# Top-32 attention: the mask of every head item from ScalarE's Sign, the flag checked in the next item's last search step

## The chip, the core and the metric

The kernel runs on one core of one Trainium2 chip. The metric is the device time of one launch in microseconds; its median over three runs is 2931.31 us (2930.16 to 2934.05). The core has TensorE (PE, matrix products), VectorE (DVE), ScalarE (ACT), GpSimd (POOL) and SyncE (SP, which starts transfers). Each engine works through its own list of instructions in order; the lists meet only in semaphores.

## The reference, cut to what matters

Four batches of 512 tokens (256 wide) pass four layers: a cross-attention with 16 heads, a mixture of eight experts, a second cross-attention block, and a self-attention with gated values. The change concerns the attention inside the third layer. For each batch and each of four heads, every token scores 1601 context rows and keeps the 32 largest:

```
Q = (x_text @ Wq).reshape(Bb, Tt, H, DH)
K = (x_vision @ Wk).reshape(Bb, Gg, H, DH)
scores = jnp.einsum('bthd,bghd->bhtg', Q, K) / np.sqrt(DH).astype(np.float32)
scores = jnp.where(vision_mask[:, None, None, :], scores, -jnp.inf)
topv, topi = jax.lax.top_k(scores, K_TOP)
probs = jax.nn.softmax(topv, axis=-1)
bi = jnp.arange(Bb)[:, None, None, None]
hi = jnp.arange(H)[None, :, None, None]
ti = jnp.arange(Tt)[None, None, :, None]
attn = jnp.zeros_like(scores).at[bi, hi, ti, topi].set(probs)
attn_mean = attn.mean(axis=1)
V = x_vision @ Wv
c_t = jnp.einsum('btg,bgd->btd', attn_mean, V)
c_t = c_t * text_mask[..., None]
```

The rest of the layer (a film modulation, a long convolution by a discrete Fourier transform, a feed-forward net, layer norms) follows it and is not touched.

## The kernel before

The attention is worked in **items**. A batch has four tiles of 128 tokens, and with four heads 16 items, n = 0 to 15, tile n // 4 and head n % 4. A token is a partition, the 1601 scores of a head lie along the free axis. The order on each engine is written out by hand; per batch a semaphore gets a fixed number of increments, and `nth(b, sem, k)` is its value at the k-th of batch b.

An item passes the engines like this.

- **TensorE** computes scores in steps of half a pair of heads (`scores`, lines 1549 and 1552), four steps ahead of the item. ScalarE copies them to `s_sb` (`score_out`, line 1053).
- **VectorE** searches the scores for the 32 largest in two stages. `search(n, k)`, line 2331, takes the eight largest of 27 parts of 60 scores, in seven portions k = 0 to 6; these 216 candidates are those of the *next* item. Between the portions, the loop over k takes the eight largest of the candidates of the *present* item (line 2346) and strikes them out (line 2348), alternately: four times the one, three times the other. After k = 6 the last of the 32 is the threshold `least`.
- For an **even** item, VectorE works out a bias from the threshold (lines 2361 to 2364: `NEG`, minus the row's maximum, and `under`, minus the number just below the threshold). ScalarE makes the mask with the function Sign (line 1095): +1 where a score reaches the threshold, -1 elsewhere, and the row sum with it. For an **odd** item VectorE makes the mask itself (line 2370), 1 or 0, with the row sum; of the threshold only `NEG` is computed (line 2366).
- **ScalarE** also computes the exponentials of all 1601 scores (line 1090), those of the 32 largest with their sum (line 1096), and, in `scale_head` (line 1073), Relu of the masked exponentials times the weight.
- **TensorE** adds the row sums over the partitions (`count`, line 1563). ScalarE copies the number to `kept` (line 1101): it is the **flag**. If all rows kept exactly 32, the mask is good.
- **VectorE** reads the flag into a register (`settle`) and branches; a slow repair stands in the branch. Then `weight` (lines 2317 and 2319) computes the weight from the sum.
- **GpSimd** multiplies the exponentials by the mask (line 847) as soon as the weight is there, and adds scaled heads to the mean over the heads (line 839). For items 14 and 15 VectorE does this work itself (lines 2381 and 2383).
- When a tile's four heads are added up, TensorE turns the mean (line 1573), ScalarE copies it (lines 874 and 870, in items 7, 11 and 15 and once behind the loop), and TensorE multiplies it with v (line 1581) in two parts; ScalarE copies the result (line 1057).

Where the flag is checked differs. The flag of an even item n is checked at the end of item n+1, behind VectorE's mask. The flag of an odd item n is checked in item n+1 at k = 4. ScalarE writes the flag before `scale_head` in odd items and behind it in even items. Buffers: `s_sb` has six slots, `probs1` three, `kept01` (the mask) and `kept_by_row` two, `under` one.

## Time and profile before

| | |
|---|---|
| Median of three runs | 2931.31 us |
| The profiled execution, its own time | 2937.11 us |
| Its span | 2935.3 us |
| Busy in the span: PE, DVE, ACT, POOL | 2303.0, 1464.4, 1459.0, 917.4 us |
| Top-32 stage, first batch (1206.0 to 1338.4 us) | 132.4 us |
| The same stage in the other three batches | 130.7, 130.7, 133.0 us |
| Mean granted TensorE clock over the span | 0.881 |

A row of a timeline gives the start in the span, the duration, the engine, the line of the kernel, the operation with the tiles that it writes and reads, how many instructions the row holds, and in brackets how long the engine had been idle before it and which engine's instruction ended the wait. Durations of neighbours overlap a little, as the next instruction starts before the last one's results are written; the distance between starts is what an instruction costs its engine.

### The profile page before, as it was taken

The numbers are of one execution on the slowest core, as the hardware profiler recorded it, in microseconds if no ns is written. First come the engines' busy times: TensorE is split into PE (matmuls) and PEld (weight loads), VectorE is DVE, ScalarE is ACT, GpSimd is POOL, SyncE is SP. The second block draws the span as 40 slices with busy tenths as digits, with TensorE's granted clock in tenths as the row PEclk, the third lists the DMA queues.
The fourth block names the chain that finished last, engine by engine and source line by source line (L and its number), as shares of the span: only waits on it lengthen the run. The fifth ranks groups of instructions, "written<-read, shape, count | busy, mean of one in ns | idle before, by whom it ended". The sixth has DMA issues, their size and how long they took to land.

```text
span 2935.3 us, 36676 instructions
## 1 busy us (share of the span) xinstructions
PE 2303.0 (78%) x12668; PEld 1303.1 (44%) x12668; DVE 1464.4 (50%) x4388; ACT 1459.0 (50%) x2266; POOL 917.4 (31%) x473
## 2 busy tenths in 40 slices
PE   0566899999974998568888668997668898668997
PEld 0532232323222665346555346555346555346555
DVE  8656112121221111696653696553696553696553
ACT  2144577687750222481365571365571365571374
POOL 1023000100102111372094371094371094270094
PEclk9988899999986999668998769998769998769999
DMA  2045844344152111103022103022103022103022
GB/s 61 0 150 174 156 62 77 46 76 65 38 181 60 45 45 41 44 1 119 1 46 43 46 1 119 1 52 41 43 1 119 0 49 41 39 1 112 0 30 44
DMA packets 176516, 166.51 MB, mean 57 GB/s; under 512 B 84048, under 2 KB 147152, under 8 KB 176304
## 3 DMA queue, kind: packets, MB, share of 16 engines
q1 hardware_dynamic: 168816, 154.73, 22.5%
q0 software_dynamic: 7504, 9.35, 1.7%
q8 instruction: 102, 1.67, 0.3%
q14 instruction: 94, 0.77, 0.1%
HBM read 131.88 MB, written 32.32 MB: 56 GB/s over the span
## 4 chain that ended last, share of the span: by engine, by line
PE 46%; DVE 22%; POOL 11%; issue 8%; ACT 7%; DMA 4%; SPq 2%; DVEq 1%; POOLq 0%; ACTq 0%
PE ps L1300 5%; POOL sb_arena L726 5%; PE ps L1311 5%; DVE sb_xnT L2331 5%; POOL sb_xtn L724 4%; ACT sb_arena L958 3%; PE ps L1581 2%; PE ps L1482 2%; PE ps L1702 2%; PE ps L1495 2%; PE ps L1650 2%; PE ps L1501 2%; PE ps L1720 2%; PE ps L1630 2%; PE ps L1639 2%
## 5 line engine op out<-in xcount | busy, mean ns | idle before, releaser
L958 ACT ACTIVATE sb_arena<-ps 128x1024 f32<-128x1024 f32 x416 | 402.7, 1021 | 125.7 <-PE ps L1300 116.7
L2331 DVE MAX8 sb_xnT<-sb_arena 128x8 f32<-128x60 f32 (+1 forms) x1728 | 246.7, 205 | 72.2 <-ACT sb_arena L1053 72.2
L1300 PE MATMUL ps<-sb_arena 96*128 96x512 bf16 x832 | 236.2, 390 | 29.8 <-ACT sb_arena L958 15.7
L2492 DVE TENSOR_REDUCE sb_arena<-ps 128x2 f32<-128x1024 f32 x128 | 156.2, 1223 | 203.1 <-PE ps L1720 202.7
L1549 PE MATMUL ps<-sb_arena,sb_xnT 32*128 32x400 f32 (+1 forms) x512 | 166.0, 735 | 109.5 <-ACT sb_arena L1053 105.9
L847 POOL TENSOR_TENSOR sb_arena<-sb_arena 128x1601 f32<-128x1601 f32 x56 | 176.3, 3148 | 202.3 <-DVE sb_arena L2319 197.1
L1311 PE MATMUL ps<-sb_arena 128*32 128x512 f32 x1664 | 226.4, 617 | 1.4 <-ACT sb_arena L958 1.4
L726 POOL TENSOR_TENSOR sb_arena<-sb_arena,sb_xtn 128x1024 f32<-128x1024 f32 (+1 forms) x112 | 208.6, 1862 | 8.8
L782 POOL DMA_INDIRECT taken_rows<-sb_taken,sb_slots x32 | 31.3, 979 | 553.8 <-DVEq L2097 545.2
L1138 ACT ACTIVATE sb_arena<-ps 128x512 f32<-128x512 f32 x256 | 152.0, 594 | 89.9 <-PE ps L1688 89.6
L724 POOL TENSOR_TENSOR sb_arena<-sb_arena 128x1024 f32<-128x1024 f32 (+1 forms) x16 | 24.1, 1505 | 536.5 <-DVEq L2449 531.2
L1144 ACT ACTIVATE sb_arena<-ps,sb_arena 128x512 f32<-128x512 f32 x256 | 176.3, 689 | 28.0 <-DVE sb_arena L2492 19.7
L724 POOL TENSOR_TENSOR sb_xtn<-sb_arena 128x1024 f32<-128x1024 f32 (+1 forms) x112 | 176.0, 1571 | 8.8
L1300 PEld LDWEIGHTS ps<-sb_arena 96*128 96x128 bf16 x832 | 57.8, 98 | 240.5 <-ACT sb_arena L958 207.9
L1688 PEld LDWEIGHTS ps<-sb_ident,sb_arena 128*128 128x128 f32 x1024 | 111.2, 142 | 111.7 <-issue 67.7
L1688 PE MATMUL ps<-sb_ident,sb_arena 128*128 128x128 f32 x1024 | 145.7, 283 | 10.3 <-ACT sb_arena L1144 10.1
L1702 PE MATMUL ps<-sb_arena 128*64 128x128 f32 x2048 | 141.3, 281 | 15.4 <-POOLq L860 15.4
L1720 PE MATMUL ps<-sb_arena 64*128 64x512 f32 x512 | 146.5, 652 | 2.7 <-ACT sb_arena L1130 2.7
L1019 ACT ACTIVATE sb_arena<-ps 128x512 f32<-128x512 f32 x39 | 23.3, 597 | 220.6 <-PE ps L1495 220.6
L839 POOL TENSOR_TENSOR sb_arena<-sb_arena 128x1601 f32<-128x1601 f32 x40 | 129.7, 3242 | 8.8 <-ACT sb_arena L1073 8.8
L984 ACT ACTIVATE sb_ln_std<-sb_ln_mv,sb_eps 128x1 f32<-128x1 f32 x48 | 14.1, 294 | 236.0 <-DVE sb_ln_mv L2004 212.1
L1549 PEld LDWEIGHTS ps<-sb_arena,sb_xnT 32*128 32x128 f32 x512 | 61.9, 265 | 154.3 <-ACT sb_arena L1053 108.4
(350 smaller groups left out, 4665.0 us busy)
## 6 DMA issues: line engine op xcount, KB each, us to landing
sb_arena<-k_spill SPq DMA_DIRECT2D x96, 208.0 KB, 7.9
sb_arena<-in_ctxT SPq DMA_DIRECT2D x12, 1601.0 KB, 7.2
sb_arena<-in_dft SPq DMA_DIRECT2D x5, 2048.0 KB, 7.6
k_spill<-sb_arena SPq DMA_DIRECT2D x12, 832.0 KB, 5.2
sb_arena<-in_w SPq DMA_DIRECT2D x16, 512.0 KB, 7.1
sb_arena<-in_idft SPq DMA_DIRECT2D x4, 2048.0 KB, 8.7
sb_arena<-in_wf SPq DMA_DIRECT2D x8, 1024.0 KB, 12.1
o_rows<-sb_arena SPq DMA_DIRECT2D x32, 256.0 KB, 2.3
```

The lines of the kernel that those rows point to most:

```text
L724: link(eng.tensor_tensor(heads(tmp[:, :, 0:nh * D2] if e else v2[:, :, hs]), src, mix, ALU.mult))
L726: link(eng.tensor_tensor(v2[:, :, hs], v2[:, :, hs], tmp[:, :, 0:nh * D2], ALU.add))
L847: G.tensor_tensor(e, e, kept01[:, n % 2, 0:GKEYS], ALU.mult).then_inc(p1_kept, 1)
L958: A(probs0[:, 2 * (m % 4):2 * (m % 4) + 2, :], ps[:, 2 * (m % 2):2 * (m % 2) + 2, :], ACT.Exp).then_inc(pair_probs, 1)
L1144: A(p2[:, n % 4, :], ps[:, S2_BANKS[n % 4], :], ACT.Exp, bias=nmax2[:, t, h:h + 1], accum_out=sums2[:, t, h:h + 1]).then_inc(p2_ready, 1)
L1300: ins = mm(ps[:, 2 * (m % 2) + i, :], k_stack[0:NSPLIT, h, k * P:(k + 1) * P], q_stack[0:NSPLIT, h, :], start=True, stop=True)
L1311: ins = mm(ps[32 * j:32 * j + 32, 4 + q % 2, :], v0s[b % 2][:, k, h * V0W:(h + 1) * V0W], probs0[:, (4 * g + j) % 8, :], start=(k == 0), s ...
L1549: mm(ps[:, 2 * j + i, 0:w], q1[r, t * P:(t + 1) * P], kT1[r, c0:c0 + w], start=True, stop=False)
L1688: ins = tr(ps[:, 2 + n % 2, j * P:(j + 1) * P], p2[:, n % 4, j * P:(j + 1) * P], ident[:, :])
L1702: ins = mm(ps[j * D2:(j + 1) * D2, 4 + pair % 2, t * P:(t + 1) * P], v2[:, k, h * D2:(h + 1) * D2], pT2[:, (2 * s + j) % 4, k * P:(k + 1) ...
L1720: mm(ps[:, S2_BANKS[n % 4], :], q2[half, pair, t * P:(t + 1) * P], kT2[half, pair, :], start=True, stop=True).then_inc(s2_done, 1)
L2331: ins = V.max(cand[:, n % 2, 8 * j:8 * j + 8], s_sb[:, n % 6, c0:c0 + w])
```

## The change

Every item's mask comes from ScalarE's Sign, in slot n % 2 of `kept01`, with its row sum; VectorE's own mask and its semaphore `choice_ready` are gone. VectorE works out the bias of every item (four operations on one column), and `under` has two slots, which moves the tiles behind it by three words. All flags compare with the same number. Flag and weight of item n are dealt with in item n+1 at k = 6, between the last maximum of the eights and the last portion of the search, for even and odd items alike. On ScalarE every item has the order Exp, Sign, small Exp, `scale_head(n - 1)`, copy of the flag. TensorE and GpSimd wait for the one semaphore `sign_ready`.

```diff
--- before.py
+++ after.py
@@ -36,7 +36,7 @@
 ICH = INNER // P
 
 H1, D1, TOPK = 4, 32, 32
-ALL_DECIDED = [int(np.float32(P * n).view(np.int32)) for n in (GKEYS - 2 * TOPK, TOPK)]
+ALL_DECIDED = [int(np.float32(P * n).view(np.int32)) for n in (GKEYS - 2 * TOPK, GKEYS - 2 * TOPK)]
 HALF_ULP = 2.0 ** -24
 DROPPED = -3.4e38
 STEPS = [((0, 400), (400, 400)), ((800, 401), (1201, 400))]
@@ -248,7 +248,7 @@
         s_cut = at(o, [KS]); o += KS
         kept01 = at(o, [2, KS], BF16); o += KS
         kept_by_row = at(o, [2, 1]); o += 2
-        under = at(o, [3]); o += 3
+        under = at(o, [2, 3]); o += 6
         probs1 = at(o, [3, KS]); o += 3 * KS
         p_mean = at(o, [2, KS]); o += 2 * KS
         attnT = at(o, [KCH, P]); o += KCH * P
@@ -457,8 +457,7 @@
         top_ready = sem("top_ready", 16)
         e1_ready = sem("e1_ready", 16)
         sum1_ready = sem("sum1_ready", 16)
-        choice_ready = sem("choice_ready", 8)
-        sign_ready = sem("sign_ready", 8)
+        sign_ready = sem("sign_ready", 16)
         count_ready = sem("count_ready", 16)
         count_done = sem("count_done", 16)
         w1_ready = sem("w1_ready", 16)
@@ -841,8 +840,7 @@
                 for n in range(TILES * H1 - 2):
                     e = probs1[:, n % 3, 0:GKEYS]
                     pool.wait_ge(e1_ready, nth(b, e1_ready, n + 1))
-                    if n % 2 == 0:
-                        pool.wait_ge(sign_ready, nth(b, sign_ready, n // 2 + 1))
+                    pool.wait_ge(sign_ready, nth(b, sign_ready, n + 1))
                     pool.wait_ge(w1_ready, nth(b, w1_ready, n + 1))
                     G.tensor_tensor(e, e, kept01[:, n % 2, 0:GKEYS], ALU.mult).then_inc(p1_kept, 1)
                     if n >= 1:
@@ -1088,19 +1086,17 @@
                         probs_used(n - 3)
                     bias = stat1[:, n % 3, NEG:NEG + 1]
                     A(probs1[:, n % 3, 0:GKEYS], s_sb[:, n % 6, 0:GKEYS], ACT.Exp, bias=bias).then_inc(e1_ready, 1)
-                    if n % 2 == 0:
-                        if n >= 2:
-                            act.wait_ge(count_done, nth(b, count_done, n - 1))
-                            act.wait_ge(p1_kept, nth(b, p1_kept, n - 1))
-                        A(kept01[:, 0, 0:GKEYS], s_sb[:, n % 6, 0:GKEYS], ACT.Sign, bias=under[:, 2:3], accum_out=kept_by_row[:, 0, :]).then_inc(sign_ready, 1)
+                    if n >= 2:
+                        act.wait_ge(count_done, nth(b, count_done, n - 1))
+                        act.wait_ge(p1_kept, nth(b, p1_kept, n - 1))
+                    A(kept01[:, n % 2, 0:GKEYS], s_sb[:, n % 6, 0:GKEYS], ACT.Sign, bias=under[:, n % 2, 2:3],
+                      accum_out=kept_by_row[:, n % 2, :]).then_inc(sign_ready, 1)
                     A(top_e[:, n % 2, :], top[:, n % 2, :], ACT.Exp, bias=bias,
                       accum_out=stat1[:, n % 3, SUM:SUM + 1]).then_inc(sum1_ready, 1)
-                    if n % 2 == 0 and n >= 1:
+                    if 1 <= n < TILES * H1 - 1:
                         scale_head(n - 1)
                     act.wait_ge(count_done, nth(b, count_done, n + 1))
-                    A(kept[0:1, n:n + 1], ps[0:1, 7, 3 * P:3 * P + 1], ACT.Copy, scale=1.0 if n % 2 else -1.0).then_inc(count_ready, 1)
-                    if n % 2 and n < TILES * H1 - 1:
-                        scale_head(n - 1)
+                    A(kept[0:1, n:n + 1], ps[0:1, 7, 3 * P:3 * P + 1], ACT.Copy, scale=-1.0).then_inc(count_ready, 1)
                     if n % H1 == 1 and n > 2 * H1:
                         context_out(n // H1 - 2)
                 context_out(TILES - 2)
@@ -1554,10 +1550,7 @@
 
                 def count(n):
 
-                    if n % 2 == 0:
-                        pe.wait_ge(sign_ready, nth(b, sign_ready, n // 2 + 1))
-                    else:
-                        pe.wait_ge(choice_ready, nth(b, choice_ready, n // 2 + 1))
+                    pe.wait_ge(sign_ready, nth(b, sign_ready, n + 1))
                     if n >= 1:
                         pe.wait_ge(count_ready, nth(b, count_ready, n))
                     ins = mm(ps[0:1, 7, 3 * P:3 * P + 1], kept_by_row[:, n % 2, :], ones[:, :], start=True, stop=True)
@@ -2347,7 +2340,7 @@
                         else:
                             ins = V.match_replace(c, eights[:, 8 * r:8 * r + 8], c, DROPPED)
                         ins.then_inc(cand_step, 1)
-                        if k == 4 and n >= 1 and n % 2 == 0:
+                        if k == 6 and n >= 1:
                             settle(n - 1)
                             weight(n - 1)
                         search(n + 1, k)
@@ -2355,21 +2348,13 @@
                     if n >= 3:
                         dve.wait_ge(p1_scaled, nth(b, p1_scaled, n - 2))
                     least = eights[:, TOPK - 1:TOPK]
-                    if n % 2 == 0:
-                        if n >= 2:
-                            dve.wait_ge(sign_ready, nth(b, sign_ready, n // 2))
-                        V.tensor_scalar(st[:, NEG:NEG + 1], eights[:, 0:1], -1.0, None, ALU.mult)
-                        link(V.tensor_scalar(under[:, 0:1], least, -HALF_ULP, None, ALU.mult))
-                        link(V.tensor_scalar(under[:, 1:2], least, HALF_ULP, under[:, 0:1], ALU.mult, ALU.max))
-                        V.tensor_scalar(under[:, 2:3], under[:, 1:2], least, None, ALU.subtract).then_inc(top_ready, 1)
-                    else:
-                        V.tensor_scalar(st[:, NEG:NEG + 1], eights[:, 0:1], -1.0, None, ALU.mult).then_inc(top_ready, 1)
-                        if n >= 3:
-                            dve.wait_ge(p1_kept, nth(b, p1_kept, n - 1))
-                            dve.wait_ge(count_done, nth(b, count_done, n - 1))
-                        V.tensor_scalar(kept01[:, 1, 0:GKEYS], s, least, 0.0, ALU.is_ge, ALU.add, accum_out=kept_by_row[:, 1, :]).then_inc(choice_ready, 1)
-                        settle(n - 1)
-                        weight(n - 1)
+                    bound = under[:, n % 2, :]
+                    if n >= 2:
+                        dve.wait_ge(sign_ready, nth(b, sign_ready, n - 1))
+                    V.tensor_scalar(st[:, NEG:NEG + 1], eights[:, 0:1], -1.0, None, ALU.mult)
+                    link(V.tensor_scalar(bound[:, 0:1], least, -HALF_ULP, None, ALU.mult))
+                    link(V.tensor_scalar(bound[:, 1:2], least, HALF_ULP, bound[:, 0:1], ALU.mult, ALU.max))
+                    V.tensor_scalar(bound[:, 2:3], bound[:, 1:2], least, None, ALU.subtract).then_inc(top_ready, 1)
 
                 mean = p_mean[:, (TILES - 1) % 2, 0:GKEYS]
                 for n in (NH - 2, NH - 1):
```

## Rows read from the trace of the kernel before

**Rows 1.** Busy time of each engine in the first batch's top-32 stage.

```profile
core 0: us, PE busy (x) PEld busy (x) DVE busy (x) ACT busy (x) POOL busy (x), PEclk, DMA share, GB/s
...
1206.00:1338.40 132.40, 84.53 (x433) 55.45 (x431) 121.77 (x684) 97.18 (x135) 82.52 (x28) 0.68 0.06 19
```

**Rows 2.** Timeline of ScalarE: flag 0, items 2, 9, 11, last context copies.

```profile
1224.81 0.16 ACT L1101 ACTIVATE sb_arena<-ps 1x1 f32<-1x1 f32 x1
...
1234.47 1.63 ACT L1090 ACTIVATE sb_arena<-sb_arena 128x1601 f32<-128x1601 f32 x1 [0.53 <-DVE sb_arena L2364]
...
1236.01 1.62 ACT L1095 ACTIVATE sb_arena<-sb_arena 128x1601 bf16<-128x1601 f32 x1
...
1237.62 0.31 ACT L1096 ACTIVATE sb_xnT<-sb_arena 128x32 f32<-128x32 f32 x1
...
1237.92 1.61 ACT L1073 ACTIVATE sb_arena<-sb_arena 128x1601 f32<-128x1601 f32 x1
...
1239.44 0.14 ACT L1101 ACTIVATE sb_arena<-ps 1x1 f32<-1x1 f32 x1
...
1289.82 0.16 ACT L1101 ACTIVATE sb_arena<-ps 1x1 f32<-1x1 f32 x1 [2.77 <-PE ps L1563]
...
1299.01 1.48 ACT L1053 ACTIVATE sb_arena<-ps 128x1600 f32<-128x1600 f32 x1
...
1300.39 1.52 ACT L874 ACTIVATE sb_arena<-ps 128x512 f32<-128x512 f32 x3
...
1301.98 1.61 ACT L1090 ACTIVATE sb_arena<-sb_arena 128x1601 f32<-128x1601 f32 x1
...
1349.73 0.38 ACT L1057 ACTIVATE sb_arena<-ps 128x256 f32<-128x256 f32 x1 [8.16 <-PE ps L1581]
...
1784.82 0.38 ACT L1057 ACTIVATE sb_arena<-ps 128x256 f32<-128x256 f32 x1 [6.16 <-PE ps L1581]
```

**Rows 3.** Timeline of VectorE: items 2, 10, 11, 14 and 15.

```profile
1234.22 0.21 DVE L2364 TENSOR_SCALAR sb_arena<-sb_arena 128x1 f32<-128x1 f32 x1
...
1290.84 0.17 DVE L2317 RECIPROCAL sb_arena<-sb_arena 128x1 f32<-128x1 f32 x1 [1.52 <-ACT sb_arena L1101]
...
1291.17 0.58 DVE L2331 MAX8 sb_xnT<-sb_arena 128x8 f32<-128x60 f32 x4
...
1292.79 0.55 DVE L2331 MAX8 sb_xnT<-sb_arena 128x8 f32<-128x60 f32 x4
...
1293.26 0.14 DVE L2361 TENSOR_SCALAR sb_arena<-sb_arena 128x1 f32<-128x1 f32 x1
...
1293.74 0.21 DVE L2364 TENSOR_SCALAR sb_arena<-sb_arena 128x1 f32<-128x1 f32 x1
...
1298.60 0.37 DVE L2346 MAX8 sb_arena<-sb_xnT 128x8 f32<-128x216 f32 x1
...
1322.26 0.21 DVE L2364 TENSOR_SCALAR sb_arena<-sb_arena 128x1 f32<-128x1 f32 x1
...
1325.50 0.15 DVE L2366 TENSOR_SCALAR sb_arena<-sb_arena 128x1 f32<-128x1 f32 x1
...
1325.60 1.88 DVE L2370 TENSOR_SCALAR_CACHE_REDUCE sb_arena<-sb_arena 128x1601 bf16<-128x1601 f32 x1
...
1328.79 0.16 DVE L2317 RECIPROCAL sb_arena<-sb_arena 128x1 f32<-128x1 f32 x1 [1.31 <-issue]
```

**Rows 4.** Timeline of TensorE: context products, counts 9 and 15, last turns.

```profile
1281.77 5.92 PE L1581 MATMUL ps<-sb_arena 128*128 128x128 f32 x26
...
1289.59 0.19 PE L1563 MATMUL ps<-sb_ones,sb_arena 128*1 128x1 f32 x2
...
1329.59 0.19 PE L1563 MATMUL ps<-sb_ones,sb_arena 128*1 128x1 f32 x2 [0.66 <-ACT sb_arena L870]
...
1338.48 1.87 PE L1573 MATMUL ps<-sb_ident,sb_arena 128*128 128x128 f32 x10 [2.70 <-DVE sb_arena L2383]
...
1766.80 0.19 PE L1563 MATMUL ps<-sb_ones,sb_arena 128*1 128x1 f32 x2 [0.64 <-ACT sb_arena L870]
```

**Rows 5.** Timeline of GpSimd: the mask product of one item.

```profile
1286.09 3.25 POOL L847 TENSOR_TENSOR sb_arena<-sb_arena 128x1601 f32<-128x1601 f32 x1 [1.07 <-DVE sb_arena L2319]
```

## The prediction

> **What bounds the kernel now.** I read the windows first. The change touches only the top-32 attention that each of the four batches runs once. In the first batch that stage lasts 132.4 us, and VectorE is busy for 121.8 of them, ScalarE for 97.2, GpSimd for 82.5 and TensorE for 84.5, at a mean granted clock of 0.68 [rows 1]. So VectorE looks saturated (92%) and ScalarE looks as if it had room (73%). The other three batches repeat the pattern, so I work one out and take it four times.
>
> Shares don't show what sets the pace of an item, so next I read the timelines of ScalarE and VectorE item by item. I call S(n) the start of the operation at line 2364 that hands item n's threshold to ScalarE. S(2) is 1234.22 and S(14) is 1322.26 [rows 3]: twelve items in 88.04 us, 7.34 each. Even and odd items differ. In an even item VectorE's chain is the 27 partial maxima with the eights between them, with a check of the previous flag in the middle. In an odd item the check stands behind the 1.88 us mask of line 2370 [rows 3], and by then the flag is long there.
>
> Last I read what one flag check costs where nothing hides it. ScalarE's copy of the count (line 1101) starts at 1289.82 [rows 2], and VectorE's reciprocal behind the check starts at 1290.84, after 1.52 us idle put down to that copy [rows 3]. That is 1.02 us from the start of the copy to the first operation behind the branch. The check that follows the last mask shows 1.31 us of idle with no engine as its releaser [rows 3]; this is the dearest price I have.
>
> **What the change removes.** In each odd item the mask leaves VectorE (1.88 us) and three operations on one column come in. From line 2361 to line 2364 takes 0.48 us [rows 3]. VectorE therefore gets some 1.3 us per odd item back. ScalarE gets eight more Signs per batch: Sign to Relu is 1.91 us, of which the small Exp between them is 0.3, so 1.6 us each [rows 2]. Both Signs read one table with Exp and Relu: the even items show Exp, Sign, Relu and copy back to back with no load between them [rows 2].
>
> **What it moves, and the new loop.** Every flag is now checked in the next item's last search step, and ScalarE writes the flag only behind Exp, Sign, the small Exp and the Relu of the previous item. Now VectorE cannot finish threshold n+1 before it has seen flag n, and ScalarE cannot start item n+1 before it has the threshold. Step by step, from S(n):
>
> - 0.25 to the Exp (1234.22 to 1234.47), 1.54 to the Sign, 1.91 to the Relu, 1.52 to the copy: the copy starts at S+5.22 [rows 2, 3].
> - 1.02 to the reciprocal, 0.33 to the maxima held back behind it (1290.84 to 1291.17), 0.47 for the last four maxima (1292.79 to 1293.26), 0.48 to the next S [rows 3].
>
> Sum: 7.52 us per item against 7.34 now. Without the flag VectorE would be faster: the seventh maximum of the eights starts at S+4.86 (1293.74 to 1298.60) and takes 0.28, so the reciprocal could start at S+5.14 instead of S+6.24 [rows 3]. VectorE thus idles 1.1 us in every item where it now idles in some even ones; the freed 1.3 us turn into that wait. Behind the waiting VectorE stand the last search step, the threshold and so ScalarE's whole next item; GpSimd's mask product, which waits for the weight, comes later too but is covered (below).
>
> In items 7 and 11 ScalarE turns the previous tile's rows first: score copy 1.38 and four small copies 1.59 (1299.01, 1300.39, 1301.98) [rows 2]. From the start of the copy that makes 0.05+1.38+1.59 = 3.02, against 2.55 until S+0.25. So 0.47 twice a batch, 0.94.
>
> **The sum of one batch.** Start: flag 0 is copied at 1224.81 [rows 2], so S(1) = 1224.81+1.02+0.33+0.47+0.48 = 1227.11, and S(2) = 1234.63, 0.41 later than now [rows 3]. Middle: 12 x 7.52 + 0.94 = 91.2, so S(14) = 1325.8, now 3.55 late. Item 15 has no search behind it; now it takes only 3.24 (1322.26 to 1325.50 [rows 3]), while the new loop without the maxima takes 7.05, so S(15) = 1332.9. End: Sign 15 must be over before TensorE's count 15, 0.25+1.54+1.7 after S(15), at 1336.4; now count 15 goes at 1329.59 [rows 4]. That is 6.8 us late.
>
> Part of it comes back. Now TensorE waits for VectorE's last sum with the final turns (2.70 idle before 1338.48) in the first batch, and from count 15 to the end of ScalarE's last copy it is 20.5 us (1329.59 to 1349.73+0.38); in the second, with no such gap, 18.4 (1766.80 to 1784.82+0.38) [rows 2, 4]. Afterwards no last mask and no late check stand in VectorE's way, so the gap goes. 18.4 is the upper end. The lower is 15.7, an estimate: 20.5 less its 2.7 us gap, and less the 2.1 us by which the second batch's stretch is the shorter one, since TensorE may then run its first products as fast as in the first batch and its last as fast as in the second. I take 17.1, the middle, against a mean of 19.5 now: 2.4 back. Net 6.8 - 2.4 = 4.4 us.
>
> For the check I take 1.3 instead of 1.02 in one case of five: 15 x 0.2 x 0.3 = 0.9. So 5.3 us per batch, 21 us in all. The sum was made against the profiled run (2937.1 us, span 2935.3). The median shown is 5.8 us lower, 0.2%; I put the difference on the median: 2931.3 + 21 = 2952 us.
>
> **What I cost at nothing.** The Relu needs GpSimd's product. Its wait ends with the weight, some 0.6 us behind the reciprocal (two operations of 0.2 and the start), and the product takes 3.25 [rows 5]: it ends at 6.24+0.6+3.25 = S+10.1, that is 2.6 into the next item, and the Relu wants it at 3.70. Cover 1.1 us; beyond that each us of delay adds one to every item. The wider `under` shifts the tiles behind it by 12 bytes; no row shows a price for that, and whatever it does to GpSimd lies under the same cover. TensorE's count n waits behind the scores: now copy 9 waits because 5.92 us of context products stand ahead (1281.77, count 9 at 1289.59) [rows 4]. The later item 9 covers that by about 1 us; at the low clock the scores ahead of it can use this up, at most some 2.7 us a batch, 0 at the other end. I take 0.
>
> **The Trainium skill.** The windows show VectorE at 92% and ScalarE at 73% of the stage [rows 1]. The Trainium skill, Perfetto Trace Analysis, section Optimizing Scalar/DVE Operations, says that a saturated DVE may be relieved by giving work to Scalar. By that rule alone the stage would get shorter, as in the first rival below. This trace does show that VectorE is nearly full; it shows as well that its operations wait for ScalarE's flag, which the rule leaves out.
>
> **The rivals.**
>
> *Engine load decides (faster).* If the check did not hold VectorE, its own item would take 4.86+0.28+0.33+0.47+0.48 = 6.42 and ScalarE's 4.97+0.05+1.38 = 6.40, plus 1.59 in one item of four: 6.8. Twelve items save 12 x (7.34-6.8) = 6.5 us, item 15 loses little and the end gains 2.4; with the later start about -7 per batch, -28 in all: 2903 us. For it speaks the load. Against it stands the place of the copy: the check is free only if the copy starts 1.1 us sooner, by S+4.12, and Exp, Sign, small Exp and Relu, back to back, already take until S+5.22. It decides only if the Relu falls out from ahead of the copy, which the code doesn't do. Chance 7%.
>
> *No difference.* The loop comes out at 7.34, 0.18 shorter than my sum, by a quicker check, and the end returns more than I take: within 5.9 us of 2931. Every stalled check I found costs 1.02 or more, so 8%.
>
> *TensorE or GpSimd late too.* The counts behind context products (up to 2.7 us a batch) or the product for the Relu run out of cover, or every check costs 1.3 (15 x 0.3 = 4.5 a batch, minus the 0.9 taken: +14): 2963 to 2975 us. Chance 13%. In here is also a mask that goes to the slow repair branch; the branch's wide searches don't show in the trace of before, and a score one step under the threshold would be needed.
>
> **How the numbers follow.** My case has 72%: 2952, with its own range 2941 to 2963 (loop 0.05 either way: 3; end 1.4 either way per batch: 6; checks all at 1.02: -4, two in five at 1.3: +4). Slower therefore 72+13 = 85%, same 8%, faster 7%; 0.2%, or 5.9 us, is about what a measurement can tell from no change. The range for 8 in 10 leaves out the faster case and the upper half of the late one: 2938 to 2966.
>
> **What the new profile would show.** Line 2370 is gone, line 1095's Sign comes 64 times. S to S is 7.5 in plain items, even and odd alike, 8.0 in items 7 and 11. Before each reciprocal VectorE idles about 1.1 us, released by the copy. ScalarE idles about 1.1 us before each big Exp, released by the threshold. The stage is 4 to 6 us longer, VectorE's busy time in it 10 us shorter. I am wrong if the idle before the reciprocal is short or put to another engine, if the copy waits for TensorE's count, or if the Relu waits for GpSimd.

## The result, and the profile after

The changed kernel takes 2967.86 us (median of four runs, 2964.36 to 2973.66), the kernel before 2932.0 us beside it (four runs, 2930.16 to 2934.05). The ratio is 1.0124, 95% interval [1.0105, 1.0143]: slower by 36 us. I had predicted 2952 us, 21 us slower, with 2966 us as the upper end. The profiled execution took 2973.66 us (span 2971.9), 36.55 us more than the one of before.

The page of the changed kernel gives busy time per engine in the first line. The second is the group of the big Exp: count, busy time and mean ns of one, and the idle time of ScalarE just before them with what ended it.

```profile
PE 2324.8 (78%) x12668; PEld 1311.9 (44%) x12668; DVE 1421.9 (48%) x4420; ACT 1506.6 (51%) x2330; POOL 918.3 (31%) x473
...
L1088 ACT ACTIVATE sb_arena<-sb_arena 128x1601 f32<-128x1601 f32 x64 | 104.2, 1629 | 62.3 <-DVE sb_arena L2357 62.3
```

VectorE did 42.5 us less and ScalarE 47.6 us more, as the change intends. ScalarE now waits 62.3 us for thresholds ahead of its big Exps, about 1 us for each of the 64 items. Line 2357 is the last operation of the threshold (line 2364 before), 1088 the big Exp, 1092 the Sign, 1094 the small Exp, 1071 the Relu, 1099 the copy of the flag, 1051 the copy of the scores, 1055 the copy of a context, 2310 and 2312 the reciprocal and the weight behind the check, 845 GpSimd's product, 1556 the count, 1566 the turns, 1574 the product with v.

ScalarE in item 2, with the start of item 3, then in items 6 and 7 of the changed kernel (timeline, to be set beside [rows 2]):

```profile
1237.49 1.63 ACT L1088 ACTIVATE sb_arena<-sb_arena 128x1601 f32<-128x1601 f32 x1 [1.01 <-DVE sb_arena L2357]
1239.03 1.62 ACT L1092 ACTIVATE sb_arena<-sb_arena 128x1601 bf16<-128x1601 f32 x1
...
1240.94 1.61 ACT L1071 ACTIVATE sb_arena<-sb_arena 128x1601 f32<-128x1601 f32 x1
1242.46 0.14 ACT L1099 ACTIVATE sb_arena<-ps 1x1 f32<-1x1 f32 x1
1242.51 1.48 ACT L1051 ACTIVATE sb_arena<-ps 128x1600 f32<-128x1600 f32 x1
1245.02 1.63 ACT L1088 ACTIVATE sb_arena<-sb_arena 128x1601 f32<-128x1601 f32 x1 [1.03 <-DVE sb_arena L2357]
...
1274.33 1.53 ACT L872 ACTIVATE sb_arena<-ps 128x512 f32<-128x512 f32 x3
...
1275.92 1.61 ACT L1088 ACTIVATE sb_arena<-sb_arena 128x1601 f32<-128x1601 f32 x1
```

VectorE in items 2 and 3, and the checks of flags 5 and 7 (timeline, to be set beside [rows 3]):

```profile
1237.24 0.21 DVE L2357 TENSOR_SCALAR sb_arena<-sb_arena 128x1 f32<-128x1 f32 x1
...
1243.48 0.16 DVE L2310 RECIPROCAL sb_arena<-sb_arena 128x1 f32<-128x1 f32 x1 [1.01 <-ACT sb_arena L1099]
...
1244.77 0.21 DVE L2357 TENSOR_SCALAR sb_arena<-sb_arena 128x1 f32<-128x1 f32 x1
...
1266.38 0.16 DVE L2310 RECIPROCAL sb_arena<-sb_arena 128x1 f32<-128x1 f32 x1 [1.35 <-issue]
...
1281.89 0.16 DVE L2310 RECIPROCAL sb_arena<-sb_arena 128x1 f32<-128x1 f32 x1 [1.49 <-ACT sb_arena L1099]
```

Here is the loop. The threshold is handed over at 1237.24; Exp, Sign, small Exp and Relu follow back to back; the flag is copied at 1242.46; VectorE stands idle for 1.01 us and goes on at 1243.48; the next threshold leaves at 1244.77. That is 7.53 us from threshold to threshold. Each engine waits about 1 us for the other in a plain item, so neither is full. In item 7 the turned rows (line 872) stand ahead of the Exp and take the place of its idle time.

All fifteen steps from threshold to threshold, first batch, us (measured at each item's first threshold operation, worked out from the timelines):

```
before 10.43 8.53 6.09 8.51 6.08 8.55 6.09 8.51 6.09 9.60 6.09 8.16 6.09 8.17 3.73
after  12.22 7.52 7.53 7.54 7.50 7.86 7.50 8.00 7.53 7.50 7.72 7.78 7.83 7.51 7.34
```

GpSimd's product of the same item starts behind the weight and is over at 1247.30, 1.2 us before the Relu that wants it starts (1248.47). No Relu of the stage waits for GpSimd.

```profile
1244.07 3.23 POOL L845 TENSOR_TENSOR sb_arena<-sb_arena 128x1601 f32<-128x1601 f32 x1 [4.31 <-DVE sb_arena L2312]
```

The end of the stage on TensorE and on ScalarE (timelines, to be set beside [rows 4] and the last lines of [rows 2]):

```profile
1339.98 0.19 PE L1556 MATMUL ps<-sb_ones,sb_arena 128*1 128x1 f32 x2 [4.24 <-issue]
...
1348.94 1.61 PE L1566 MATMUL ps<-sb_ident,sb_arena 128*128 128x128 f32 x13 [0.56 <-ACT sb_arena L1055]
```

```profile
1348.42 0.38 ACT L1055 ACTIVATE sb_arena<-ps 128x256 f32<-128x256 f32 x1 [8.05 <-PE ps L1574]
...
1357.56 0.39 ACT L1055 ACTIVATE sb_arena<-ps 128x256 f32<-128x256 f32 x1 [6.16 <-PE ps L1574]
```

Count 15 goes at 1339.98 and the last context copy ends at 1357.95, 17.97 us later, where it was 20.5 before. The last turns no longer wait for VectorE, as predicted; they wait for ScalarE's copy of the context before last.

Two windows of the changed kernel: the stage, from the first threshold to the last context copy, and the stretch behind it from the first feed-forward product (line 1643) to the first row maximum of the next attention.

```profile
1217.50:1357.95 140.45, 87.72 (x450) 60.13 (x448) 102.23 (x625) 107.61 (x148) 84.31 (x28) 0.64 0.07 20
1406.90:1489.00 82.10, 74.77 (x222) 41.86 (x224) 42.18 (x72) 26.66 (x44) 7.17 (x4) 0.92 0.01 2
```

The same feed-forward stretch of the kernel before:

```profile
1399.10:1477.30 78.20, 70.89 (x222) 39.93 (x224) 42.16 (x71) 26.63 (x43) 7.11 (x4) 0.96 0.01 2
```

The diff touches nothing in this stretch. TensorE runs the same 222 products, in 74.77 us instead of 70.89, at a granted clock of 0.92 instead of 0.96. That is 3.9 us that my sum didn't have.

The whole execution cut at landmarks gives the account. "First context product" is the first product of a batch's third layer (line 1522 before). Sums over the four batches, us; the single batches of the stage are in brackets:

```
stretch                                        before                    after
start to the first context product             1160.3                    1162.5
first context product to first threshold       161.2                     165.6
stage: first threshold to last context copy    536.6 (134.9 133.1        561.4 (140.5 140.1
                                                      135.4 133.3)              140.4 140.4)
from there to the first feed-forward product   196.0                     196.0
feed-forward product to first row maximum      318.7 (78.2 79.9          325.8 (82.1 82.1
                                                      80.7 79.9)                79.8 81.8)
first to last row maximum                      421.7                     422.8
last row maximum to last output sum            138.3                     135.2
```

The stages are 24.8 us longer. The other 11.7 of the 36.5 us lie where the diff changes nothing.

### The profile page after: what moved, and what is told of

Read it like the earlier page. It is cut to its first block, busy times and chain, and to the rows that moved or that the text cites. A ratio compares the mean times of both kernels' runs of the same rounds, so it can differ in the third digit from the quotient of the medians.

```text
span 2971.9 us, 36772 instructions
## 1 busy us (share of the span) xinstructions
PE 2324.8 (78%) x12668; PEld 1311.9 (44%) x12668; DVE 1421.9 (48%) x4420; ACT 1506.6 (51%) x2330; POOL 918.3 (31%) x473
## 4 chain that ended last, share of the span: by engine, by line
PE 45%; DVE 15%; ACT 11%; issue 11%; POOL 10%; DMA 4%; SPq 2%; DVEq 1%; POOLq 0%; ACTq 0%; another core or an unknown queue 0%
PE ps L1296 5%; POOL sb_arena L725 5%; PE ps L1307 5%; POOL sb_xtn L723 4%; ACT sb_arena L1092 3%; ACT sb_arena L956 3%; PE ps L1643 2%; PE ps L1478 2%; PE ps L1695 2%; PE ps L1491 2%; PE ps L1497 2%; PE ps L1713 2%; PE ps L1574 2%; PE ps L1623 2%; PE ps L1632 2%
## 5 line engine op out<-in xcount | busy, mean ns | idle before, releaser
L1545 PE MATMUL ps<-sb_arena,sb_xnT 32*128 32x400 f32 (+1 forms) x512 | 173.3, 766 | 92.9 <-ACT sb_arena L1051 89.3
L781 POOL DMA_INDIRECT taken_rows<-sb_taken,sb_slots x32 | 31.3, 978 | 555.5 <-DVEq L2090 546.9
L1134 ACT ACTIVATE sb_arena<-ps 128x512 f32<-128x512 f32 x256 | 152.0, 594 | 91.2 <-PE ps L1681 90.9
L1088 ACT ACTIVATE sb_arena<-sb_arena 128x1601 f32<-128x1601 f32 x64 | 104.2, 1629 | 62.3 <-DVE sb_arena L2357 62.3
```

What stands on the lines that cost most here:

```text
L1545: mm(ps[:, 2 * j + i, 0:w], q1[r, t * P:(t + 1) * P], kT1[r, c0:c0 + w], start=True, stop=False)
```

## The experiments

"The flag loop" is my theory: the next threshold waits for the check of the last flag, which waits for ScalarE, which waits for the threshold. Its first rival is load: ScalarE has 1.6 us more in every second item. Two questions came up on the way: what the stretches outside the stage have to do with it, and what set the pace of the kernel before. Each ratio is to the kernel before, run on the same chip. "Untouched" is the sum of four rows of the table that the diff doesn't touch: first context product to first threshold, and the last three. It is 1039.9 before and 1049.4 after. The row ahead of them (start to the first context product) isn't touched either and is left out; it varies by itself, from 1151 to 1160 us between two profiles of the kernel before.

**The changed kernel again** (no edit). 

> The changed kernel once more, unaltered. In its first profile the four attention stages (from the first threshold to the last context copy) are 24.8 us longer together than before, and the other 11.8 us lie in stretches that the diff does not touch. If these 11.8 us are a chance of one execution, this profile shows the stages 24 to 26 us longer again and the rest within 3 us of before, and the median is some 25 us above before (2957). If they are a consequence of the change, the rest is 8 to 14 us longer here too and the median stays near 2968.

2961.86 us against 2924.61, ratio 1.012 [1.0095, 1.0145]. The stages sum to 561.7 us (561.4 in the first profile), untouched 1047.3. So the loss is a property of the kernel, and so is its split, within 2 us.

**The layout alone**, in the kernel before:

```diff
-        under = at(o, [3]); o += 3
+        under = at(o, [3]); o += 6
```

> The kernel before with only the three words of space that the wider under takes, so all tiles behind it lie 12 bytes further. Theory that the 12 bytes cost nothing on the path: 2932, ratio 1.000 within 0.002. Rival, that the shift is the unexplained 11 us (TensorE, ScalarE or GpSimd reading tiles that lie worse): 2940 to 2944.

2925.77 us, ratio 1.0 [0.9985, 1.0015]; stages 534.4, untouched 1040.3. The 12-byte shift costs nothing, and it isn't what slows the untouched stretches.

**A longer stage without the change.** The kernel before with one more pass of VectorE ahead of the thresholds of items 4, 8 and 12, its result unused:

```diff
+                    if n in (4, 8, 12):
+                        V.tensor_scalar(s_cut[:, 0:GKEYS], s, 0.0, None, ALU.is_ge)
```

> The kernel before with one more VectorE pass over 1601 scores (1.9 us, result not used) ahead of the thresholds of items 4, 8 and 12, and nothing else. It lengthens each stage by about 5.6 us with idle of TensorE, as the change does, 22 us in all. Theory A, that a longer pause of TensorE lowers its granted clock in the stretches behind the stage: the total grows by more, 30 to 36 us, and the stretch between feed-forward and scores shows a lower clock as in the changed kernel (0.92 against 0.96). Theory B, that only the stage counts: +20 to +24 us, 2952 to 2956.

2953.27 us, ratio 1.0096 [1.0076, 1.0116]. The pass didn't have the size that I had assumed (1.9 us). VectorE, timeline, the passes of items 4, 8 and 12 in the first batch:

```profile
1246.88 1.55 DVE L2356 TENSOR_SCALAR sb_arena<-sb_arena 128x1601 f32<-128x1601 f32 x1
...
1277.92 1.23 DVE L2356 TENSOR_SCALAR sb_arena<-sb_arena 128x1601 f32<-128x1601 f32 x1
...
1308.24 3.49 DVE L2356 TENSOR_SCALAR sb_arena<-sb_arena 128x1601 f32<-128x1601 f32 x1
```

One instruction takes 1.23, 1.55 or 3.49 us. GpSimd, what starts during or ahead of them:

```profile
1247.54 3.77 POOL L847 TENSOR_TENSOR sb_arena<-sb_arena 128x1601 f32<-128x1601 f32 x1
...
1278.26 4.00 POOL L847 TENSOR_TENSOR sb_arena<-sb_arena 128x1601 f32<-128x1601 f32 x1
...
1307.86 3.01 POOL L847 TENSOR_TENSOR sb_arena<-sb_arena 128x1601 f32<-128x1601 f32 x1
1310.84 4.31 POOL L839 TENSOR_TENSOR sb_arena<-sb_arena 128x1601 f32<-128x1601 f32 x1
```

Each pass ends 0.89 us (0.89 to 0.91 in all twelve of the execution) after GpSimd changes from one instruction to the next: 1246.88 + 1.55 = 1247.54 + 0.89, 1277.92 + 1.23 = 1278.26 + 0.89, and 1308.24 + 3.49 = 1310.84 + 0.89. So its length is what is left of GpSimd's instruction, and 0.89 more; and the GpSimd instruction that starts then takes 3.77 to 4.31 us, where before those of line 847 take 3.0 to 3.3 and those of line 839 3.0 to 3.6.

The stages sum to 548.3 us, 12 to 17 us over the three profiles of the kernel before (536.6, 534.4 and 531.6), but the timed loss is 28.7 us. The profiled execution (span 2943.3) was the lowest of this kernel's runs, and I can't reconcile the two. Part of it is luck of that execution: its third batch's last pass took only 1.11 us, and that stage is 3 us shorter than the other three. A longer stage didn't bring the slow feed-forward stretch with it here (316.5 us in all, 318.7 before). More than that this run doesn't decide.

**The flag first.** The changed kernel with the copy of the flag ahead of the Relu and the score copy. No work is added or taken away, so load is the same and only the loop is shorter:

```diff
-                    if 1 <= n < TILES * H1 - 1:
-                        scale_head(n - 1)
                     act.wait_ge(count_done, nth(b, count_done, n + 1))
                     A(kept[0:1, n:n + 1], ...)
+                    if 1 <= n < TILES * H1 - 1:
+                        scale_head(n - 1)
```

> The changed kernel, but ScalarE copies the count to the flag ahead of the Relu of the previous item (scale_head) instead of behind it. My theory, that the loop from threshold over the flag back to the next threshold is what costs: the copy then starts some 1.1 us sooner, at S+4.1, VectorE's idle before the reciprocal goes from 1.0 us to under 0.5, an item takes 6.8 to 6.9 us instead of 7.52, the stage shrinks by some 8 us against the changed kernel, and the total is 30 to 40 us under it, at or a little under the time of before (2915 to 2935). Rival, that ScalarE's load (eight more Signs per batch) is what costs: the time stays within 8 us of the changed kernel.

2925.11 us against 2926.96, ratio 0.9994 [0.998, 1.0008]: the whole loss is gone. The stages sum to 530.1 us, 31.3 less than in the changed kernel, and the untouched stretches to 1039.3. ScalarE, item 3 and the first instruction of item 4:

```profile
1235.87 1.62 ACT L1088 ACTIVATE sb_arena<-sb_arena 128x1601 f32<-128x1601 f32 x1
...
1239.89 0.16 ACT L1097 ACTIVATE sb_arena<-ps 1x1 f32<-1x1 f32 x1 [0.48 <-PE ps L1556]
1239.96 1.63 ACT L1071 ACTIVATE sb_arena<-sb_arena 128x1601 f32<-128x1601 f32 x1
1241.50 1.49 ACT L1051 ACTIVATE sb_arena<-ps 128x1604 f32<-128x1604 f32 x1
1242.88 1.62 ACT L1088 ACTIVATE sb_arena<-sb_arena 128x1601 f32<-128x1601 f32 x1
```

VectorE, the reciprocals behind flags 2 and 3:

```profile
1234.06 0.16 DVE L2310 RECIPROCAL sb_arena<-sb_arena 128x1 f32<-128x1 f32 x1
...
1240.93 0.16 DVE L2310 RECIPROCAL sb_arena<-sb_arena 128x1 f32<-128x1 f32 x1 [0.36 <-issue]
```

Now the Exp at 1242.88 has no idle time before it: ScalarE is full, with 7.01 us from Exp to Exp (1235.87 to 1242.88), and 0.48 of that is its wait for TensorE's count, which nothing covers any more. Plain items take 6.6 to 7.3 us, items 7 and 11, where the turns come in, 7.9 to 8.5. Load as the cause of the loss is refuted: with the same load the kernel is level with before. It isn't faster either, for now ScalarE's load, with that wait, sets the pace.

**The masks alone.** The changed kernel with the checks and the order of the copies of before, so that only the second mask's engine differs:

```diff
-                        if k == 6 and n >= 1:
+                        if k == 4 and n >= 1 and n % 2 == 0:
 ...
                     V.tensor_scalar(bound[:, 2:3], ...).then_inc(top_ready, 1)
+                    if n % 2:
+                        settle(n - 1)
+                        weight(n - 1)
```

and on ScalarE the Relu ahead of the flag in even items, behind it in odd ones.

> One half of the change: all masks by Sign, but every flag checked where it was checked before (flag of an odd item in the middle of the next search, flag of an even item behind the odd item's threshold), and ScalarE's copy ahead of the Relu in odd items as before. My theory: no loss from the Signs. An odd item takes 6.4 to 6.6 us, an even one 7.5 to 8.0 with 1.0 to 1.5 us of idle in its middle, a pair 14.0 to 14.4 against 14.6 now, total 2915 to 2930. Rival, that the Signs on ScalarE cost: 2945 or more.

2942.89 us, ratio 1.0062 [1.0045, 1.0078]. I expected a gain, and this is a clear miss. The plain steps are those of the kernel before (8.54 and 6.09 us). So 1.3 us less of VectorE's work in every odd item bought nothing. Items 2 to 4 show why. Lines 1547 and 1558 are here the scores and the count, 2312 and 2359 the reciprocal and the last threshold operation. ScalarE:

```profile
1234.80 0.14 ACT L1099 ACTIVATE sb_arena<-ps 1x1 f32<-1x1 f32 x1
1234.85 1.48 ACT L1051 ACTIVATE sb_arena<-ps 128x1600 f32<-128x1600 f32 x1
...
1240.24 0.16 ACT L1099 ACTIVATE sb_arena<-ps 1x1 f32<-1x1 f32 x1 [0.48 <-PE ps L1558]
```

TensorE:

```profile
1236.38 1.71 PE L1547 MATMUL ps<-sb_arena,sb_xnT 32*128 32x401 f32 x4 [3.07 <-ACT sb_arena L1051]
...
1240.02 0.19 PE L1558 MATMUL ps<-sb_ones,sb_arena 128*1 128x1 f32 x2
```

VectorE:

```profile
1229.58 0.21 DVE L2359 TENSOR_SCALAR sb_arena<-sb_arena 128x1 f32<-128x1 f32 x1
...
1236.52 0.16 DVE L2312 RECIPROCAL sb_arena<-sb_arena 128x1 f32<-128x1 f32 x1 [0.64 <-issue]
...
1241.28 0.16 DVE L2312 RECIPROCAL sb_arena<-sb_arena 128x1 f32<-128x1 f32 x1 [0.95 <-ACT sb_arena L1099]
...
1244.18 0.21 DVE L2359 TENSOR_SCALAR sb_arena<-sb_arena 128x1 f32<-128x1 f32 x1
```

The even threshold (1229.58) is followed by its flag after 5.22 us. The score copy frees TensorE for the next scores, the odd count stands behind them in TensorE's queue, and the odd flag comes 5.44 us after the even one. The check takes 1.04, the rest of the search 2.90. Together they are the 14.60 us of the pair. A loop through a flag sets this pair too; it runs through TensorE's scores. VectorE's idle ahead of the two reciprocals takes up most of what the mask freed. The kernel before has the same loop, at flag 3:

```profile
1244.89 0.16 ACT L1101 ACTIVATE sb_arena<-ps 1x1 f32<-1x1 f32 x1 [2.09 <-PE ps L1563]
```

```profile
1245.92 0.16 DVE L2317 RECIPROCAL sb_arena<-sb_arena 128x1 f32<-128x1 f32 x1 [0.44 <-issue]
```

Flag 3 comes 5.45 us behind flag 2 (1239.44 in [rows 2]), ScalarE waits 2.09 us for the count, and the reciprocal follows 1.03 us behind the copy, the price of a check that waits. The loss has two places. Items 7 and 11 take 9.6 to 10.0 us, where the kernel before has 8.2 to 8.5: their Sign has to stand behind the turned copies, and VectorE's mask had no such queue ahead of it. Items 9 and 13 give part of it back, so that from first to last threshold it is 3.1 us over the four batches. The other 6.7 of the stages' 9.8 us (546.4 against 536.6) lie behind the last threshold, where Sign 15 now stands on ScalarE ahead of the last count. So the Signs aren't free where they stand in that order. The untouched stretches are 1044.2 us.

**The checks alone.** The kernel before with its masks, and every check at the new place:

```diff
-                        if k == 4 and n >= 1 and n % 2 == 0:
+                        if k == 6 and n >= 1:
 ...
-                        settle(n - 1)
-                        weight(n - 1)
```

> The other half: the masks as before (VectorE makes the odd ones), but every flag is checked at k = 6 of the next item. My theory: in odd items VectorE idles 1.1 us for the flag of the even item, which ScalarE writes behind its Relu, and the check is no longer hidden behind the mask of 1.9 us; a pair takes 15.4 to 16.0 us instead of 14.6, +5 to +10 us per batch, total 2955 to 2970. Rival, that moving the check is harmless and the masks cost: within 6 us of 2932.

2954.43 us, ratio 1.0098 [1.0078, 1.0118]; stages 558.4, untouched 1042.5. VectorE, the reciprocals behind flags 2 and 3:

```profile
1233.63 0.16 DVE L2317 RECIPROCAL sb_arena<-sb_arena 128x1 f32<-128x1 f32 x1 [1.02 <-ACT sb_arena L1101]
...
1241.48 0.17 DVE L2317 RECIPROCAL sb_arena<-sb_arena 128x1 f32<-128x1 f32 x1
```

From even to odd the step is 7.5 us, the flag loop (1.02 idle for the copy). From odd to even it is 7.85 with no idle time put down to the flag: there VectorE's mask of 1.87 us and the check in its own chain make the length. Moving the checks alone costs the stages 22 to 27 us, four fifths or more of what the whole change costs them. Taking the mask off VectorE as well doesn't give that back, since the loop then holds all items at 7.5.

**The kernel before again** (no edit). 

> The kernel before, unaltered, as a control with a profile of its own on the chip of the next three. Ratio 1.000 within 0.002; sum of the four stages 534 to 537 us; the stretch from the feed-forward's first GELU to the first row maximum of the last attention (untouched by the diff) 318 us over the four batches, as in the two profiles of this code so far (318.7, and 318.0 with only the layout moved), if that sum belongs to the kernel and not to the execution.

2923.51 us against 2925.16, ratio 0.9992 [0.9981, 1.0004]. Stages 531.6 (I had expected 534 to 537), untouched 1035.0. With this profile and that of the layout run there are three of the unchanged work: stages 534.2 on average, untouched 1038.4 (1035.0 to 1040.3). The changed kernel's two have 561.5 and 1048.4. By these means the change costs 27.3 us in the stages and 10.0 outside them, together 37 us, the timed difference. (The stretch ahead of the first context product is 3 us longer too, and the profiled spans differ by 40; that row alone varies by 9 us between two profiles of the kernel before.)

**Does a longer stage slow what follows?** The kernel before with one maximum over a score row ahead of item 2's threshold, and with three (range(3) in the second kernel):

```diff
+                    if n == 2:
+                        for i in range(1):
+                            V.max(s_cut[:, 8 * i:8 * i + 8], s)
```

> The kernel before with one more maximum over 1601 scores on VectorE (about 1.8 us, result not used) ahead of item 2's threshold, once a batch: the stage becomes longer by one idle of TensorE and is otherwise the same. Linear theory: the total grows by 4 x 1.8 = 7 us. Theory of the clock: TensorE's granted clock in the stretches behind the stage changes with the moment at which they begin, so the total differs from +7 by several us either way, and the difference lies in the untouched stretches at a different granted clock.

> The same with three such maxima, about 5.4 us a batch, as long as the change makes the stage. Linear theory: +21.6 us. If a longer stage as such lowers the clock behind it (as the changed kernel's untouched stretches, 7 us longer, suggest): +28 to +36 us. By the theory that only the moment counts: anything from +15 to +35, with no order by length between this and the run with one maximum.

VectorE, the added operation:

```profile
1222.92 1.81 DVE L2357 MAX8 sb_arena<-sb_arena 128x8 f32<-128x1601 f32 x1
```

Each adds 1.73 us to one step of a batch, so 6.9 and 20.7 us in all. The stages grow by less: they sum to 534.1 and 547.2 us, against 534.2 on average before, for the step behind item 9, 9.2 to 10.0 us before, takes only 8.2 to 8.9 in both. Measured: ratios 1.0017 [1.0006, 1.0028] and 1.0059 [1.0045, 1.0074], that is 6 and 17 us. Untouched 1042.8 and 1039.9. With three, a stage 3.3 us longer per batch, half of the change's 6.8, leaves what follows within the spread of the kernel before. With one, a stage of the old length leaves it 2.5 us above that spread. What follows doesn't go by the stage's length.

**The same delays in the changed kernel.** If its extra 10 us are fixed to it, the delays add their own size. If they depend on the moment at which the stage hands over, the sum comes out lower.

> The changed kernel with the same three maxima ahead of item 2's threshold. Linear theory: 21.6 us over the changed kernel, so some 57 us over before (ratio 1.0195). If the changed kernel's stretches behind the stage only meet a bad moment, moving the moment by 5.4 us gives part of it back: +45 to +52 us over before (1.015 to 1.018).

> The changed kernel with one maximum more ahead of item 2's threshold (+1.7 us a batch, 7 us in all). Linear theory: +42 us over before (1.0144), the untouched stretches between the stages stay at 1047 to 1050 us over the four batches, as in the two profiles of the changed kernel. Theory of the moment: the untouched stretches come to 1039 to 1044, as in the kernels before and in the run with three maxima (1041), and the total to +34 to +38 (1.0115 to 1.013).

With three: 2977.93 us, ratio 1.0181 [1.0164, 1.0199]; stages 581.5, untouched 1041.1. With one: 2971.38 us, 1.013 [1.0112, 1.0147]; stages 568.3, untouched 1045.0. The stages grow by the delay (20 and 7 us). The timed ratios would be 1.0195 and 1.0148 if everything added up, from 1.0124; both are lower, but the first lies within its interval and the second just outside, and 1.0124 has an interval of its own. The untouched stretches are shorter than the changed kernel's 1048.4 in both. A stage that is another 5 us per batch longer doesn't make them longer. That leans to the moment, and doesn't settle it.

**Hand over first, check later.** The flag-first kernel, with the check and the weight behind the handed-over threshold, to beat both kernels by taking the check out of the loop:

```diff
-                        if k == 6 and n >= 1:
-                            settle(n - 1)
-                            weight(n - 1)
 ...
                     V.tensor_scalar(bound[:, 2:3], ...).then_inc(top_ready, 1)
+                    if n >= 1:
+                        settle(n - 1)
+                        weight(n - 1)
```

> The kernel of e4 (all masks by Sign, flag copied ahead of the Relu), and VectorE hands item n's threshold to ScalarE before it checks flag n-1 and works out its weight. Theory, that only the loop through the flag costs and the Signs do not: neither the flag nor the check then stands between two thresholds, item 1 no longer waits for flag 0 (1.8 us a batch), ScalarE's own 6.5 to 6.9 us an item set the pace, 8 in the items that turn a tile. Stages 515 to 525 us together, total 2905 to 2917, ratio 0.993 to 0.997. Rival, that GpSimd's product for the Relu now comes too late (it starts with the weight, some 1.3 us behind the threshold, and takes 3.0 to 3.2): ScalarE waits up to 1 us ahead of each Relu and the time stays at that of e4, 0.999.

2944.5 us against 2933.73, ratio 1.0041 [1.0025, 1.0057]. A second miss. VectorE, the last threshold operation of an item (line 2354) and the reciprocal behind the check (line 2310):

```profile
1239.04 0.21 DVE L2354 TENSOR_SCALAR sb_arena<-sb_arena 128x1 f32<-128x1 f32 x1
1239.89 0.16 DVE L2310 RECIPROCAL sb_arena<-sb_arena 128x1 f32<-128x1 f32 x1 [0.64 <-issue]
```

The flag had long been there (ScalarE's copy at 1236.39), and VectorE still stood 0.64 us, put to no other engine. In the kernel before, the check of an even item's flag stands behind the 1.88 us mask and mostly costs no idle time. Here nothing lies in front of it, so an item takes 7.13 us (7.45 in about one of four, where VectorE stands 0.92 to 1.02 us instead), and VectorE's own chain sets it. That explains why the stages gain nothing. The stages sum to 534.6 us, as before; in the profile the loss lies wholly outside: untouched 1051.7. The feed-forward stretch of this kernel's first batch, and then that of the kernel before in its second profile:

```profile
1396.45:1478.60 82.15, 74.81 (x222) 41.90 (x224) 42.19 (x71) 26.67 (x44) 7.13 (x4) 0.92 0.01 2
```

```profile
1383.00:1462.85 79.85, 72.48 (x222) 40.68 (x224) 42.21 (x71) 26.68 (x44) 7.13 (x4) 0.94 0.01 2
```

With a stage of the old length this stretch is as slow as in the changed kernel, 81.9 to 82.1 us in all four batches. So it isn't the stage's length that decides.

## Why the prediction was right in its mechanism and wrong in its size

*The loop: right.* I had 7.52 us per plain item; they take 7.50 to 7.54 where the check is the cheap one. I had 8.0 for items 7 and 11; they take 8.00, 8.00, 7.99 and 8.33, and 7.78, 8.28, 8.00 and 7.98. VectorE's idle before the reciprocal is 0.99 to 1.03 us (1.1 predicted), ScalarE's before the Exp 1.01 and 1.03 (1.1 predicted). The flag-first run shows that the place of the copy does it, and that load doesn't.

*The dear check: right in kind.* I took one in five at 1.3 us. Of the 64 checks 16 cost 1.30 to 1.38, four in the first batch; one of these is the check of flag 0, which makes the first step 12.22 instead of 11.85.

*From first to last threshold: right.* My sum was 11.85 + 7.52 + 91.2 + 7.1 + 0.9 = 118.6 us per batch. Measured: 118.9, 118.5, 118.5 and 119.1, against 110.7 to 111.3 before.

*The end of the stage: 0.9 us per batch too hopeful.* I had taken 17.1 us from count 15 to the last copy, between 15.7 and 18.4. It is 17.97, 18.02, 18.30 and 17.68. The gap ahead of the last turns went as said, but the end didn't become as fast as the first batch's first products and the second's last ones together. That is 3.6 us in four batches, and the stages missed my 21 by 3.8 (24.8 against before's own profile; 27.3 between the means of the profiles).

*What I cost at nothing.* The GpSimd cover held (1.2 us left, 1.1 predicted), the layout costs nothing (1.0 [0.9985, 1.0015]), and none of the 64 copies of a flag waits for TensorE's count, so the counts behind context products stay covered.

*Where the sum ended: the step that failed.* My sum went over the stage alone (5.3 us per batch, times four), and took every other stretch as unchanged without giving a reason. They cost 10 to 12 us more; without them the time would have lain below my upper end of 2966. Most of it is in the feed-forward: 325.8 us against 318.7. What one sees there is the granted clock. Windows of 3 us around the first feed-forward products, the changed kernel's first batch:

```profile
1405.95:1408.95 3.00, 1.98 (x3) 0.95 (x4) 1.73 (x2) 2.25 (x3) 0.00 (x0) 0.54 0.00 0
1408.95:1411.95 3.00, 3.00 (x5) 1.24 (x4) 0.00 (x0) 0.69 (x1) 0.00 (x0) 0.50 0.00 0
```

and the same place in the kernel before:

```profile
1398.11:1401.11 3.00, 1.96 (x5) 1.01 (x6) 1.75 (x2) 2.27 (x3) 0.00 (x0) 1.00 0.00 0
1401.11:1404.11 3.00, 3.00 (x9) 1.33 (x8) 0.00 (x0) 1.37 (x2) 0.00 (x0) 1.00 0.00 0
```

TensorE is busy for all of the second window in both; it gets through nine matmuls at a clock of 1.00 (2.4 GHz) and five at 0.50 (1.2 GHz). These two batches are the extremes. A second dip follows 32 to 37 us behind the first product in every batch of both kernels. The granted clock sorts all 56 stretches of the fourteen profiles: without a first dip they take 78.2 to 78.4 us (7 of them), with a short one (two windows, such as 0.6 and 0.8) 79.7 to 80.7 (29), with a long one (three windows, as here) 81.3 to 82.1 (20). Of the twelve batches in the three profiles of the unchanged work two have no first dip and ten a short one. The changed kernel has a long one in three of four batches, and in two of four in its second profile; hand first in all four, flag first in none, the changed kernel's delayed versions in two each, the kernel before with one delay in two and with three in one. In the window ahead TensorE had been idle for part of the time in both batches alike (1.96 and 1.98 us busy of 3).

The layout is excluded as the cause, and the length of the stage doesn't decide it: three delays in the kernel before make the stages 13 us longer and leave the rest (1039.9), handing over first keeps them and slows the rest (1051.7). What the traces do show is an order in time. From the last context copy to the first feed-forward product all of them take 49.0 to 49.2 us. Every long dip begins 0.7 to 1.7 us ahead of that product, every short one between 0.6 us ahead of it and 1.2 us behind. So the length of the same work, 78 to 82 us, goes with whether and when the clock falls at its start. What sets that, and why the changed kernel meets the dear one more often, stays open; no run sets it and nothing else.

*The account of before: incomplete.* I read the pair of 14.6 us as VectorE's chain with a flag wait in the middle, and rested the "load" rival on 6.4 to 6.8 us per item once the mask was gone. Masks alone, and flag 3 in the trace of before, show that the pair is itself a loop through a flag and TensorE's scores. So the rule that I weighed (the Trainium skill, Perfetto Trace Analysis, section Optimizing Scalar/DVE Operations: a saturated DVE may be relieved by giving work to Scalar) would have failed here for a deeper reason than the moved check. In this kernel VectorE was busy for 92% of the stage and yet not what set its pace; moving only the mask gave 1.0062.

## What to carry to other kernels

Before a check or a read-back is moved, write down the loop through it: who produces the flag, behind what in that engine's queue, and what the consumer holds back meanwhile; an engine at 92% can still be waiting in such a loop, and work taken off it is then worth nothing. Put the flag's producer ahead of long operations that don't need it (here 31 us of stage for an edit that changes no work), and if its time of arrival allows, put the check where a long operation of its own engine stands in front of it. A sum over the changed stage alone misses what the stretches behind it do: with a clock that dips, 10 us of 2930 sat there here, so leave that much room in the range.

## What the runs showed of the hardware

- A check of a flag (a value read into a register, and a branch) costs 0.99 to 1.03 us from the start of the flag's copy to the first operation behind it in 47 of the changed kernel's 64 checks, and 1.30 to 1.38 in 16. With the flag long there and only short operations in front, VectorE stands 0.61 to 0.65 us, and 0.92 to 1.02 in about one case of four (hand first and masks alone).
- One and the same VectorE pass over 1601 columns (tensor_scalar, float32) took 1.11 to 3.49 us beside GpSimd's elementwise passes, and ended 0.89 to 0.91 us after one GpSimd instruction had given way to the next; that next one was up to 1.3 us longer. The Trainium skill, Perfetto Trace Analysis, section Optimizing Scalar/DVE Operations, says that the two engines share a read port and that a two-port VectorE operation holds it as an exclusive lock. The rows fit this, with the price added: the pass is held until the GpSimd instruction in front is over. That it is a two-port operation no run shows by itself. VectorE's mask with its row sum (1.87 to 1.89 us in all 32 cases before) shows nothing of the kind.
- The same 222 products took 70.89, 72.48, 74.77 and 74.81 us of TensorE time, at a mean granted clock of 0.96, 0.94, 0.92 and 0.92.
